# AdaLN attention and FFN on one core: softmax steps regrouped, attention given four PSUM banks of its own, one small product issued earlier

## The chip, the cores and the metric

The kernel runs on one core of one Trainium2 chip. The metric is the device time of one execution in microseconds (us). Three runs of the kernel before gave 823.74, 823.77 and 821.97 us, so the median is 823.74 us.

## The reference, cut to what matters

Input x is 32 sequences of 32 tokens of width 512, 1024 tokens in all. Everything is float32. Two residual blocks follow each other:

```
h    = cond(x)                              # per batch, a 32x32 mix of its tokens
q,k,v = h@Wq+bq, h@Wk+bk, h@Wv+bv           # 512 -> 4096, i.e. 32 heads of 128
q,k  = rms_norm(q,gq), rms_norm(k,gk)       # one norm over all 4096 columns
p    = softmax(q k^T / sqrt(128))           # 32x32 per head and sequence
x    = x + (p v) @ Wo + bo                  # 4096 -> 512
y    = causal convolution of x along the 512 features with a kernel K,
       K = 2 Re(sum_n Ct exp(dtA*l)), masked by length
x    = x + y@kernel + bias + LoRA(y)
```

## The kernel before, in words

Full precision products are made from two halves: every float32 operand is split into a rounded part ("hi", made by ScalarE) and the rest ("lo", made by VectorE), and TensorE runs hi·hi, hi·lo and lo·hi. The program is a hand-written order of instructions for each engine; the engines meet only at semaphores. An engine that waits holds back all that stands behind the wait in its own order. PSUM has eight banks of 512 floats.

The stages by the time of the profiled execution: the projections of q and k, head by head, with the raw scores (to 359 us); the value projection (359 to 518 us); attention and output projection in eight units (518 to 760 us); the convolution and the FFN (to the end).

**Value stage.** It has 28 steps, i = 7t + j with four groups t and seven products j of a Strassen scheme. In each step TensorE does two pairs of products (`value_pair`, L795 to L797). In step i VectorE makes the lo half of the weights for a later step (`split_value`, L1578), then adds each pair's result into `v_sb` (`value_post`, L1642 to L1662); at j = 0 there is nothing to add there, since ScalarE copies (`first_out`). TensorE's first product of group t needs the adds of step j = 5 of the group before (`vc22_ok`, `vu3_ok`, L1658 and L1659). Between these steps VectorE also does the inverse norms (after the adds of step 9), `soft_max(0)` (after step 11), `soft_norm(0)` (after step 13) and `spread(0)` (after step 24). GpSimd makes the weight sums of group t (`value_sums(t)`, L624 to L632) and, around them, the angle and exponent tables of the convolution kernel (`reduce_angles`, `exponents`); when all that is done it clears `p_blocks` (L683). `value_sums(t)` waits for splits 7t and 7t + 1 of VectorE.

**Softmax of a unit.** A unit n is eight heads times half of the tokens. Its work on VectorE is `soft_max(n)` (scale, row maximum, subtract: L1697, L1701, L1703), then ScalarE's exponential (`exp_scores(n)`, L1344), then `soft_norm(n)` (row sum, reciprocal, scale: L1708, L1710, L1712), then `spread(n)` (four transposes into the block matrix `p_blocks`, L1723). There is one buffer `sm_s` and one `p_blocks`: `soft_max(n)` waits for `spread(n-1)`, and `spread(n)` waits until TensorE has used `p_blocks` for unit n - 1.

**Attention of a unit.** TensorE: `attend(n)` makes eight outputs u (L1032) in four banks, `PV_BANK`, used in turn. ScalarE rounds each into `at_hi` (L1352), VectorE makes `at_lo` (L1762), and output u of unit n may start only when `at_lo` of output u - 4 is there (`alo_ok`). Then `project_first(n)` (L1049 to L1051, four groups, heads 0 to 3) and `project_second(n, g)` (L1061 to L1063, heads 4 to 7) fill banks 4 to 7, and VectorE adds bank g to `acc` (`accumulate`, L1776), which needs `wo_mm`, one count for each `project_second(n, g)`. Before an even unit the weights of the output projection are split: `split_o(m, 0)` is needed by `project_first(2m)`, `split_o(m, 1)` by `project_second(2m)` (ScalarE L1360, VectorE L1730).

**The small product.** 32 small matmuls (L1072) give the convolution kernel from `u_tab` and `expo`; they stand in front of `attend(1)`, write bank 0, and ScalarE copies the result to `k_sb` (L1403) when GpSimd has added `bo` to all of `acc` (`acc_set`). `attend(1)` waits for that copy at its third output.

VectorE's order for unit 1 in the kernel before is

```
attn_out(1); spread(2); soft_max(3); accumulate(1,(0,)); soft_norm(3)
accumulate(1,(1,)); split_o(1,0); accumulate(1,(2,3)); attn_out(2)
```

and ScalarE's is attn_out(1), exp_scores(3), split_o(1,0), attn_out(2).

Of the kernel before, what the change touches and what calls it, by code (L numbers as in the profile page):

```python
# [29 lines left out]
P = 128  # L30
# [11 lines left out]
NQ = HEADS // QUAD  # L42
OCT = 8
PAIR_BANK = (2, 4, 0, 6)
PV_BANK = (2, 3, 0, 1)
GROUP_ORDER = (3, 0, 1, 2)
UNITS = ((3, 1), (3, 0), (0, 0), (0, 1), (1, 0), (1, 1), (2, 0), (2, 1))
HG = G // 2
# [21 lines left out]
def build_program(nc, x, cond_idx, lengths, cond_w, wq, bq, wk, bk, wv, bv, wo, bo, gq, gk,  # L70
# [3 lines left out]
    with ctx:  # L74
# [19 lines left out]
        def bank(n, width=512):  # L94
            return psum[:, n * 512:n * 512 + width]
# [214 lines left out]
        def _(sp):  # L310
# [110 lines left out]
                sp.dma_start(la_nat[quadrant(c)], lora_a[:, :, P * c:P * c + P].rearrange("n r f -> r n f")).then_inc(la_in, 16)  # L421
            for c in range(KC):
                sp.dma_start(lb_nat[:, c], lora_b.rearrange("n (c p) r -> c p n r", p=P)[c]).then_inc(lb_in, 16)
            load_unit(2)
            sp.wait_ge(kern_d, 4)
            for q in range(4):
                sp.dma_start(kpad[8 * q:8 * q + 8, 0:FEAT].rearrange("h (a c) -> a h c", a=CA),
                             k_sb[32 * q:32 * q + CA]).then_inc(kpad_out, 16)
            next_weights(1)
            load_unit(3)  # L430
            load_unit(4)
# [355 lines left out]
        def _(pe):  # L787
# [221 lines left out]
            def attend(n):  # L1009


                pe.wait_ge(p_ok, n + 1)
                if n == 0:
                    pe.wait_ge(vc12_ok, 8)
                    pe.wait_ge(vc22_ok, 8)
                    pe.wait_ge(vu3_ok, 8)
                elif n == 1:
                    pe.wait_ge(vc11_ok, 8)
                    pe.wait_ge(vc21_ok, 8)
                else:  # L1020
                    pe.wait_ge(vu_in, 16 * (n - 1))
                for u in range(OCT):
                    part = (1 if u < QUAD else 0) + (2 if n == 0 else 0)
                    cols = slice(HD * (u % QUAD), HD * (u % QUAD) + HD)
                    if n == 0 and u == 2:
                        pe.wait_ge(vc21_ok, 7)
                    if not (n == 0 and u < 4):
                        pe.wait_ge(alo_ok, OCT * n + (u - 3))
                    if n == 1 and u == 2:
                        pe.wait_ge(kern_ok, 1)  # L1030
                    for g in range(HG):
                        last = mm(bank(PV_BANK[u % 4])[:, P * g:P * g + P], v_sb[:, part, g, cols], p_blocks[:, u, g, :],  # L1032
                                  start=True, stop=True)
                    last.then_inc(pv_mm, 1)

            def project_first(n):


                at_hi, at_lo = attn(n)
                pe.wait_ge(wolo_ok, 2 * (n // 2) + 1)  # L1040
                pe.wait_ge(alo_ok, OCT * n + QUAD)
                for g in range(HG):
                    if n == 0:
                        pe.wait_ge(vc21_ok, 8)
                    else:
                        pe.wait_ge(acc_ok, HG * (n - 1) + g + 1)
                    tok = slice(P * g, P * g + P)
                    for h in range(QUAD):
                        mm(bank(4 + g), at_hi[:, h, tok], wo_hi_a[:, h, :], start=(h == 0), stop=False)  # L1049
                        mm(bank(4 + g), at_hi[:, h, tok], wo_lo_a[:, h, :], start=False, stop=False)  # L1050
                        last = mm(bank(4 + g), at_lo[:, h, tok], wo_hi_a[:, h, :], start=False, stop=False)  # L1051
                last.then_inc(wo_half, 1)

            def project_second(n, g):

                at_hi, at_lo = attn(n)
                pe.wait_ge(wolo_ok, 2 * (n // 2) + 2)
                pe.wait_ge(alo_ok, OCT * n + OCT)
                tok = slice(P * g, P * g + P)
                for h in range(QUAD):  # L1060
                    mm(bank(4 + g), at_hi[:, QUAD + h, tok], wo_hi_b[:, h, :], start=False, stop=False)  # L1061
                    mm(bank(4 + g), at_hi[:, QUAD + h, tok], wo_lo_b[:, h, :], start=False, stop=False)  # L1062
                    last = mm(bank(4 + g), at_lo[:, QUAD + h, tok], wo_hi_b[:, h, :], start=False, stop=(h == QUAD - 1))  # L1063
                last.then_inc(wo_mm, 1)

            for n in range(7):
                if n == 1:
                    pe.wait_ge(tab_ok, 1)
                    pe.wait_ge(alo_ok, OCT * n)
                    for h in range(SEQ):  # L1070
                        i, q = h // 4, h % 4
                        last = mm(bank(0)[32 * q:32 * q + CA, CL * i:CL * i + CL], u_tab[:, :, 8 * q + i],  # L1072
                                  expo[:, 0:CL, 8 * q + i], start=True, stop=True, tile_position=(0, 32 * q))
                    last.then_inc(kern_mm, 1)
                attend(n)
                project_first(n)
                for g in range(HG):
                    project_second(n, g)

            def transpose_x2(g):  # L1080

                pe.wait_ge(acc_ok, HG * 6 + g + 1)
                if g >= 4:
                    pe.wait_ge(x2p_ok, g - 3)
                for c in range(KC):
                    last = nc.tensor.transpose(bank(g % 4)[:, P * c:P * c + P], acc[:, g, P * c:P * c + P], ident[:, :])
                last.then_inc(xt_mm, 1)

            attend(7)
# [84 lines left out]
        def _(act):  # L1174
# [206 lines left out]
            for i in range(1, 28):  # L1381
                t, j = i // 7, i % 7
                if j == 0:
                    split_value(i + 2)
                if i + 3 < 28 and j != 6:
                    split_value(i + 3)
                if j == 0:
                    first_out(t, 0)
                    first_out(t, 1)
                if i == 12:  # L1390
                    exp_scores(0)
                if i == 24:
                    tables()
            split_o(0, 0)


            for n in range(8):
                if n == 1:
                    act.wait_ge(kern_mm, 1)
                    act.wait_ge(acc_set, G)  # L1400
                    for q in range(4):
                        rows = slice(32 * q, 32 * q + CA)
                        last = sc.activation(k_sb[rows].rearrange("a h c -> a (h c)"), bank(0, 8 * CL)[rows, :], ACT.Copy)  # L1403
                    last.then_inc(kern_ok, 1)
                attn_out(n)
                if n % 2 == 0:
                    split_o(n // 2, 1)
                if n == 0:
                    exp_scores(1)
                if n + 2 < 8:  # L1410
                    exp_scores(n + 2)
                if n % 2 == 1 and n < 7:
                    split_o(n // 2 + 1, 0)


            def x2_out(g):

                act.wait_ge(xt_mm, g + 1)
                sc.activation(x2p[:, :, :, BPG * g:BPG * g + BPG].rearrange("p s c b -> p c b s"),
                              bank(g % 4).rearrange("p (c b s) -> p c b s", c=KC, b=BPG), ACT.Copy).then_inc(x2p_ok, 1)  # L1420

            for g in range(G):
                x2_out(g)
# [35 lines left out]
        def _(dve):  # L1459
# [276 lines left out]
            for i in range(1, 28):  # L1736
# [2 lines left out]
                    split_value(i + 2)  # L1739
                if i + 3 < 28 and j != 6:  # L1740
                    split_value(i + 3)
                if i == 27:
                    split_o(0, 0)
                if j > 0:
                    for pair in range(2):
                        value_post(t, j, pair)
                if i == 9:
                    inverse_norms()
                if i == 11:
                    soft_max(0)  # L1750
                if i == 13:
                    soft_norm(0)
                if i == 24:
                    spread(0)

            def attn_out(n):

                at_hi, at_lo = attn(n)
                for u in range(OCT):
                    h = OCT * UNITS[n][0] + u  # L1760
                    dve.wait_ge(ahi_ok, OCT * n + u + 1)
                    v.scalar_tensor_tensor(at_lo[:, u, :], bank(PV_BANK[u % 4]), params[:, PARAM["bv"], h:h + 1],  # L1762
# [2 lines left out]
            def accumulate(n, groups):  # L1765

                group, half = UNITS[n]
                for g in groups:
# [4 lines left out]
                        before = (0, 0, 1, 0, 2, 3, 4, 5)[n]  # L1773
                        dve.wait_ge(acc_ok, HG * before + g + 1)
                    at = HG * half + g
                    v.tensor_tensor(acc[:, at, :], bank(4 + g), acc[:, at, :], ALU.add).then_inc(acc_ok, 1)  # L1776

            for n in range(8):
                attn_out(n)
                if n == 0:  # L1780
                    soft_max(1)
                if n % 2 == 0:
                    split_o(n // 2, 1)
                if n == 0:
                    soft_norm(1)
                if n + 1 < 8:
                    spread(n + 1)
                if n + 2 < 8:
                    soft_max(n + 2)
                if n == 7:  # L1790
                    dve.wait_ge(lora, 2 * (2 * NLORA - 1))
                    v.transpose(a_turn[:].rearrange("p g c r -> p (g c) r"), a_sum[:].rearrange("p g (c f) -> p (g c) f", f=32)).then_inc(turned, 1)
                    v.transpose(b_turn[:].rearrange("p g c o -> p (g c) o"), b_sum[:].rearrange("p g c r -> p (g c) r")).then_inc(turned, 1)
                accumulate(n, (0,))
                if n + 2 < 8:
                    soft_norm(n + 2)
                accumulate(n, (1,))
                if n % 2 == 1 and n < 7:
                    split_o(n // 2 + 1, 0)
                accumulate(n, (2, 3))  # L1800
# [76 lines left out]
```

## Time and profile before

| what | value |
|---|---|
| profiled execution, its own time | 823.41 us |
| its span (first to last instruction) | 821.2 us |
| mean granted TensorE clock | 0.996 of full speed |
| VectorE busy | 647.0 us (79%) |
| GpSimd busy | 525.8 us (64%) |
| ScalarE busy | 327.9 us (40%) |

The span cut in 40 slices, each digit the busy share in tenths (slices 17 to 25 are the value stage, 25 to 37 attention):

```profile
PE   8799999999999999999998999999999999999998
DVE  5989898888888888987799776998998898751442
ACT  4555555555555555582223224322412421322520
POOL 4988983333333333429989997967999999910430
```

PE is TensorE, DVE VectorE, ACT ScalarE, POOL GpSimd. The 2.2 us between span and time lie outside the traced instructions.

### The profile page before, as it was taken

What the parts mean: (1) busy time and instruction counts of PE and PEld (TensorE: products, weight loads), DVE (VectorE), ACT (ScalarE), POOL (GpSimd) and SP (SyncE); (2) the same over time, 40 slices, a digit from 0 to 9 for tenths busy, and PEclk for the clock granted to TensorE, in tenths of its full rate; (3) what the DMA queues carried; (4) which work ended last, traced back from release to release, by engine and by line L of the source; (5) the groups of instructions that cost most, each with busy time, mean ns of one, the idle gap of its engine ahead of it and who ended that gap; (6) DMA issues with size and microseconds to landing.
All of it is one profiled execution on the core that took longest, in us unless ns stands there. A gap on an engine that the chain in (4) does not pass through costs nothing. (4 is left out here: it accounts for less than half of the span.)

```text
span 821.2 us, 15207 instructions
## 1 busy us (share of the span) xinstructions
PE 803.1 (98%) x6089; PEld 658.5 (80%) x6089; DVE 647.0 (79%) x652; ACT 327.9 (40%) x371; POOL 525.8 (64%) x457
## 2 busy tenths in 40 slices
PE   8799999999999999999998999999999999999998
PEld 7587888888888888888887888887888888888476
DVE  5989898888888888987799776998998898751442
ACT  4555555555555555582223224322412421322520
POOL 4988983333333333429989997967999999910430
PEclk9999999999999999999999999999999999999999
DMA  5132111111111111304433531419404724418501
GB/s 174 51 75 60 51 51 51 51 51 51 51 51 51 50 46 46 113 2 154 191 136 136 178 128 53 167 31 184 164 36 154 259 100 154 154 41 261 123 26 77
DMA packets 80703, 81.80 MB, mean 100 GB/s; under 512 B 26028, under 2 KB 61196, under 8 KB 78620
## 3 DMA queue, kind: packets, MB, share of 16 engines
q1 hardware_dynamic: 79872, 81.16, 30.9%
q8 instruction: 25, 0.41, 0.2%
q10 hardware_dynamic: 796, 0.15, 0.1%
q14 instruction: 10, 0.08, 0.0%
HBM read 64.90 MB, written 16.40 MB: 99 GB/s over the span
## 5 line engine op out<-in xcount | busy, mean ns | idle before, releaser
L494 POOL TENSOR_TENSOR w_raw<-w_raw 128x256 f32<-128x256 f32 x32 | 44.1, 1380 | 136.1 <-DMA w_raw<-in_wk 135.5
L848 PE MATMUL psum<-t_hi,w_hi 128*128 128x512 f32 x256 | 103.7, 405 | 3.2 <-DVE qk_sb L1562 1.4
L849 PE MATMUL psum<-t_lo,w_hi 128*128 128x512 f32 x256 | 99.7, 389 | 0.0
L850 PE MATMUL psum<-t_hi,w_lo 128*128 128x512 f32 x256 | 99.6, 389 | 0.0
L1313 ACT ACTIVATE sq<-qk_sb 128x1024 f32<-128x1024 f32 x31 | 32.9, 1062 | 142.9 <-issue 133.7
L1570 DVE TENSOR_TENSOR sumsq<-sumsq,sq 128x1024 f32<-128x1024 f32 x62 | 80.8, 1304 | 0.0
L848 PE MATMUL psum<-mix_hi,w_hi 128*128 128x512 f32 x192 | 74.9, 390 | 2.1 <-ACT params L1224 1.1
L850 PE MATMUL psum<-mix_hi,w_lo 128*128 128x512 f32 x192 | 74.7, 389 | 0.0
L849 PE MATMUL psum<-mix_lo,w_hi 128*128 128x512 f32 x192 | 74.7, 389 | 0.0
L1352 ACT ACTIVATE at_hi<-psum,params 128x512 fp32r<-128x512 f32 x64 | 43.9, 688 | 69.8 <-PE psum L1032 69.7
L1032 PE MATMUL psum<-p_blocks,v_sb 128*128 128x128 f32 x512 | 61.1, 281 | 3.2 <-DVE at_lo L1762 1.8
L1032 PEld LDWEIGHTS psum<-p_blocks,v_sb 128*128 128x128 f32 x512 | 60.2, 196 | 4.7 <-DVE at_lo L1762 2.0
L1476 DVE TENSOR_TENSOR w_lo<-w_raw,w_hi 128x1792 fp32r<-128x1792 f32 x30 | 61.4, 2047 | 0.0
L1203 ACT ACTIVATE w_hi<-w_raw 128x1792 fp32r<-128x1792 f32 (+2 forms) x34 | 54.8, 1611 | 13.2 <-issue 6.8
L848 PEld LDWEIGHTS psum<-t_hi,w_hi 128*128 128x128 f32 x256 | 48.0, 187 | 14.9 <-DVE t_lo L1528 2.8
L850 PEld LDWEIGHTS psum<-t_hi,w_lo 128*128 128x128 f32 x256 | 48.1, 188 | 10.5
L1762 DVE SCALAR_TENSOR_TENSOR at_lo<-psum,params,at_hi 128x512 fp32r<-128x512 f32 x64 | 47.2, 748 | 11.2 <-ACT at_hi L1352 5.2
L849 PEld LDWEIGHTS psum<-t_lo,w_hi 128*128 128x128 f32 x256 | 48.1, 188 | 8.6
L1049 PE MATMUL psum<-wo_hi_a,at_hi 128*128 128x512 f32 x128 | 50.5, 395 | 0.0
L795 PE MATMUL psum<-ring_hi,t_hi 128*128 128x512 f32 x128 | 49.9, 390 | 0.3 <-DVE v_sb L1655 0.3
L1061 PE MATMUL psum<-wo_hi_b,at_hi 128*128 128x512 f32 x128 | 50.1, 391 | 0.0
L1051 PE MATMUL psum<-wo_hi_a,at_lo 128*128 128x512 f32 x128 | 49.8, 389 | 0.0
(278 smaller groups left out, 2124.3 us busy)
## 6 DMA issues: line engine op xcount, KB each, us to landing
v_sb<-v_scr_dram SPq DMA_DIRECT2D x6, 2048.0 KB, 8.0
v_scr_dram<-v_sb SPq DMA_DIRECT2D x9, 1024.0 KB, 3.9
w_raw<-in_wq SPq DMA_DIRECT2D x32, 256.0 KB, 2.9
w_raw<-in_wk SPq DMA_DIRECT2D x32, 256.0 KB, 3.2
wv_raw<-in_wv SPq DMA_DIRECT2D x16, 512.0 KB, 4.3
toep<-kpad_dram SPq DMA_DIRECT2D x2, 4096.0 KB, 14.3
wo_raw_a<-in_wo SPq DMA_DIRECT2D x4, 1024.0 KB, 5.4
wo_raw_b<-in_wo SPq DMA_DIRECT2D x4, 1024.0 KB, 5.4
```

Source lines behind the costliest of these rows:

```text
L795: mm(out, lh, rh, start=(n == 0), stop=False)
L848: mm(bank(n), wh, hi[:, c, tok], start=(i == 0), stop=False)
L849: mm(bank(n), wh, lo[:, c, tok], start=False, stop=False)
L850: last = mm(bank(n), wl, hi[:, c, tok], start=False, stop=(i == 1))
L1032: last = mm(bank(PV_BANK[u % 4])[:, P * g:P * g + P], v_sb[:, part, g, cols], p_blocks[:, u, g, :], start=True, stop=True)
L1049: mm(bank(4 + g), at_hi[:, h, tok], wo_hi_a[:, h, :], start=(h == 0), stop=False)
L1051: last = mm(bank(4 + g), at_lo[:, h, tok], wo_hi_a[:, h, :], start=False, stop=False)
L1061: mm(bank(4 + g), at_hi[:, QUAD + h, tok], wo_hi_b[:, h, :], start=False, stop=False)
L1203: return sc.activation(w_hi[slot][:, lo:hi, :].rearrange("p b n -> p (b n)"), w_raw[slot][:, lo + 1:hi + 1, :].rearrange("p b n -> p (b n) ...
L1476: v.tensor_tensor(w_lo[slot][:].rearrange("p b n -> p (b n)"), w_raw[slot][:, 1:8, :].rearrange("p b n -> p (b n)"), w_hi[slot][:].rearran ...
L1570: v.tensor_tensor(sumsq[:, m, :], sumsq[:, m, :], sq[:, m, :], ALU.add).then_inc(total, 1)
L1762: v.scalar_tensor_tensor(at_lo[:, u, :], bank(PV_BANK[u % 4]), params[:, PARAM["bv"], h:h + 1], at_hi[:, u, :].bitcast(F32), ALU.add, ALU. ...
```

## The change

- `PV_BANK` becomes (2, 3, 4, 5); the output projection gets `O_BANK` = (0, 1, 6, 7). `attend(0)` no longer waits for `vc21_ok`. The transposes after attention use `PV_BANK` too.
- In the value stage the inverse norms, `soft_max(0)` and `soft_norm(0)` move to steps 7, 14 and 21, ahead of where that step's adds would stand (there are none); `exp_scores(0)` follows at step 16. `spread(0)` stands ahead of the adds of step 25, which is the place it had.
- VectorE's `split_o(0, 0)` moves behind the last adds of the value stage and the first four `at_lo` of unit 0.
- The small product moves between `project_first(0)` and `project_second(0)` and writes bank 4; its copy moves behind `exp_scores(1)` on ScalarE. `load_unit(2)` moves behind the writes of `kpad` in the DMA queue.
- VectorE's order for units 0 and 1 is written out, and from unit 2 on `soft_norm(n+1)` stands in unit n rather than `soft_norm(n+2)`.

```diff
-PV_BANK = (2, 3, 0, 1)
+PV_BANK = (2, 3, 4, 5)
+O_BANK = (0, 1, 6, 7)
...
-            load_unit(2)
             sp.wait_ge(kern_d, 4)
...
+            load_unit(2)
             next_weights(1)
...
-                    if n == 0 and u == 2:
-                        pe.wait_ge(vc21_ok, 7)
...
+            def kern():
+
+                pe.wait_ge(tab_ok, 1)
+                pe.wait_ge(alo_ok, OCT)
+                for h in range(SEQ):
+                    i, q = h // 4, h % 4
+                    last = mm(bank(4)[32 * q:32 * q + CA, CL * i:CL * i + CL], u_tab[:, :, 8 * q + i],
+                              expo[:, 0:CL, 8 * q + i], start=True, stop=True, tile_position=(0, 32 * q))
+                last.then_inc(kern_mm, 1)
+
             for n in range(7):
...
                 attend(n)
                 project_first(n)
+                if n == 0:
+                    kern()
...
-                if i == 12:
+                if i == 16:
                     exp_scores(0)
...
+            def kern_out():
+
+                act.wait_ge(kern_mm, 1)
+                act.wait_ge(acc_set, G)
...
             for n in range(8):
...
                 attn_out(n)
                 if n % 2 == 0:
                     split_o(n // 2, 1)
+                if n < 2:
+                    exp_scores(n + 1)
                 if n == 0:
-                    exp_scores(1)
-                if n + 2 < 8:
+                    kern_out()
+                if 0 < n < 6:
                     exp_scores(n + 2)
                 if n % 2 == 1 and n < 7:
                     split_o(n // 2 + 1, 0)
...
-                if i == 27:
-                    split_o(0, 0)
+                if i == 7:
+                    inverse_norms()
+                if i == 14:
+                    soft_max(0)
+                if i == 21:
+                    soft_norm(0)
+                if i == 25:
+                    spread(0)
                 if j > 0:
                     for pair in range(2):
                         value_post(t, j, pair)
-                if i == 9:
-                    inverse_norms()
-                if i == 11:
-                    soft_max(0)
-                if i == 13:
-                    soft_norm(0)
-                if i == 24:
-                    spread(0)
...
-            for n in range(8):
+            attn_out(0, range(QUAD))
+            split_o(0, 0)
+            attn_out(0, range(QUAD, OCT))
+            split_o(0, 1)
+            soft_max(1)
+            soft_norm(1)
+            spread(1)
+            accumulate(0, range(HG))
+            attn_out(1)
+            soft_max(2)
+            accumulate(1, (0,))
+            soft_norm(2)
+            spread(2)
+            soft_max(3)
+            accumulate(1, (1,))
+            split_o(1, 0)
+            accumulate(1, (2, 3))
+            for n in range(2, 8):
                 attn_out(n)
-                if n == 0:
-                    soft_max(1)
                 if n % 2 == 0:
                     split_o(n // 2, 1)
-                if n == 0:
-                    soft_norm(1)
-                if n + 1 < 8:
+                if n < 7:
+                    soft_norm(n + 1)
                     spread(n + 1)
                 if n + 2 < 8:
                     soft_max(n + 2)
...
-                accumulate(n, (0,))
-                if n + 2 < 8:
-                    soft_norm(n + 2)
-                accumulate(n, (1,))
+                accumulate(n, (0, 1))
```

## Rows read from the trace of the kernel before

**Rows 1.** The page's first part: busy time (share) and instructions of each engine.
```profile
PE 803.1 (98%) x6089; PEld 658.5 (80%) x6089; DVE 647.0 (79%) x652; ACT 327.9 (40%) x371; POOL 525.8 (64%) x457
```

**Rows 2.** Waits of TensorE: who waited for whom, us in total, times, longest.
```profile
PE psum L795 <- DVE v_sb L1659: 2.3, 1, 2.3
...
PE psum L1032 <- DVE at_lo L1762: 1.8, 1, 1.8
...
PE psum L1032 <- DVE v_sb L1662: 1.2, 1, 1.2
...
PE psum L795 <- DVE v_sb L1655: 0.3, 1, 0.3
```

**Rows 3.** TensorE in order of time: start, us, operation, [idle before].
```profile
518.46 2.02 PE L1032 MATMUL psum<-p_blocks,v_sb 128*128 128x128 f32 x16
...
527.08 0.48 PE L1049 MATMUL psum<-wo_hi_a,at_hi 128*128 128x512 f32 x1
...
549.03 1.14 PE L1072 MATMUL psum<-expo,prod 128*16 128x32 f32 x64
```

**Rows 4.** Stretches of time: length, busy by engine, granted clock, DMA.
```profile
437.49:447.10 9.61, 7.36 (x26) 5.79 (x26) 9.54 (x10) 2.00 (x3) 9.03 (x7) 0.82 0.54 220
...
550.10:561.40 11.30, 9.30 (x72) 8.95 (x65) 8.90 (x13) 6.69 (x12) 4.72 (x6) 0.85 1.16 156
```

**Rows 5.** The chain of waits that ended last: start, us, engine, tile, line.
```profile
434.08 3.42 DVE ring_lo L1578
437.64 2.36 POOL wv_raw L632
...
502.85 3.47 POOL p_blocks L683
...
583.43 7.27 PE psum L1032 x64
```

**Rows 6.** GpSimd in order of time, value stage.
```profile
427.33 2.41 POOL L624 TENSOR_TENSOR wv_raw<-wv_raw 128x1024 f32<-128x1024 f32 x1 [3.06 <-issue]
...
448.79 1.50 POOL L665 TENSOR_SCALAR prod<-turns 128x512 f32<-128x512 f32 x1
...
451.74 2.35 POOL L665 TENSOR_SCALAR prod<-turns 128x512 f32<-128x512 f32 x1
...
497.44 1.96 POOL L666 TENSOR_TENSOR ang<-ang,prod 128x352 f32<-128x352 f32 x1
```

**Rows 7.** VectorE in order of time, end of the value stage and units 1 and 2.
```profile
506.42 4.99 DVE L1723 STREAM_TRANSPOSE p_blocks<-sm_s 32x1024 f32<-32x1024 f32 x4 [3.53 <-POOL p_blocks L683]
...
517.10 1.21 DVE L1659 TENSOR_TENSOR v_sb<-psum,v_sb 128x1024 f32<-128x1024 f32 x1
...
563.07 4.98 DVE L1723 STREAM_TRANSPOSE p_blocks<-sm_s 32x1024 f32<-32x1024 f32 x4
...
575.31 0.69 DVE L1776 TENSOR_TENSOR acc<-psum,acc 128x512 f32<-128x512 f32 x1 [2.11 <-PE psum L1063]
...
577.55 3.48 DVE L1712 TENSOR_TENSOR sm_s<-sm_s,row_inv 128x1024 f32<-128x1024 f32 x1
...
586.07 6.14 DVE L1762 SCALAR_TENSOR_TENSOR at_lo<-psum,params,at_hi 128x512 fp32r<-128x512 f32 x8
```

**Rows 8.** Durations by line: ns min/median/max, first and last start.
```profile
L1712 DVE TENSOR_TENSOR sm_s<-sm_s,row_inv x8: 1224/1728/3479, 445.8 to 693.4; 128x1024 f32<-128x1024 f32 x8
...
L1697 DVE TENSOR_TENSOR sm_s<-scores,inv_norm x8: 1225/2275/2859, 429.4 to 683.9; 128x1024 f32<-128x1024 f32 x8
...
L1703 DVE TENSOR_TENSOR sm_s<-sm_s,row_max x8: 1226/1812/2192, 432.1 to 687.5; 128x1024 f32<-128x1024 f32 x8
...
L1730 DVE TENSOR_TENSOR wo_lo_a<-wo_raw_a,wo_hi_a x4: 2281/3113/3402, 518.2 to 695.7; 128x2048 fp32r<-128x2048 f32 x4
```

**Rows 9.** ScalarE in order of time, unit 1.
```profile
573.23 1.06 ACT L1344 ACTIVATE sm_s<-sm_s 128x1024 f32<-128x1024 f32 x1 [10.86 <-DVE sm_s L1703]
578.09 1.92 ACT L1360 ACTIVATE wo_hi_a<-wo_raw_a 128x2048 fp32r<-128x2048 f32 x1 [3.79 <-DMA wo_raw_a<-in_wo]
```

## What the change is expected to do

> **What bounds the kernel now.** I read the busy shares first: TensorE is at work for 98% of the span, VectorE for 79% [rows 1]. Nothing here makes TensorE's work shorter, since no matmul is added or dropped. So the change can only give back idle time or time at a low clock, and it can add both. Next come TensorE's waits: 2.3 us for L1659 of the value stage, 1.8 us for `at_lo`, 1.2 us for L1662, 0.3 us for L1655 [rows 2]. Then the stretches round the two long ones. At the start of group t = 2 (9.61 us) TensorE is busy for 7.36 us at a mean granted clock of 0.82: 2.25 us idle and about 0.18 x 9.61 = 1.7 us lost at the lower level, 4.0 us in all. `attend(1)` takes 11.30 us at 0.85 where the undisturbed `attend(2)` takes 7.27: 4.0 us lost, of which about 1.7 by the clock [rows 4, 5]. Last the chain of waits, which shows that the value stage has a second master beside TensorE. It runs VectorE L1578 (3.42 us), GpSimd L632 at 437.64, GpSimd without a break to its clearing of `p_blocks` (starts 502.85), VectorE's `spread(0)` and adds, TensorE [rows 5]. VectorE stood idle 3.53 us before `spread(0)`, waiting for that clearing [rows 7].
>
> **The change part by part.**
>
> Value stage. With the inverse norms at step 7, and `soft_max(0)` out of step 11, VectorE is in time for group 2, and the stall with its clock loss goes: -4.0 us at step 14. What is late next is GpSimd. Its `value_sums(2)` began at 427.33 after 3.06 us of idle time [rows 6], waiting for `split_value(14)`, and its last part waited for the 3.42 us split that stood behind `soft_max(0)`. Both splits now come in time. Its first two sums can fill that idle time, the third waits for TensorE's step 12, so L632 starts when two sums of 2.4 us are through: about 434.7 instead of 437.64, 2.9 us earlier [rows 5]. From there GpSimd is never idle until `p_blocks` is cleared. But `soft_max(0)` now lies beside it, with two operations that read SBUF twice, as the splits do. A GpSimd operation of one kind takes 1.50 or 2.35 us [rows 6]; beside 13 such VectorE operations between 440 and 503 us, nine GpSimd operations are longer than their like, from the one at 451.74 to the one at 497.44, by 7.5 us together: 0.6 us for each VectorE operation. Two more cost 1.2 us (bounds 0 and 2 x 0.86 = 1.7). The clearing ends 2.9 - 1.2 = 1.7 us earlier, while TensorE would be 4.0 us earlier, and before it had 0.3 us of wait there already. So TensorE meets a new stall of about 0.3 + 4.0 - 1.7 = 2.6 us in front of the last step. That is as long as the one removed, and I charge the same 1.7 us of clock. Gain of the stage: 1.7 - 1.7 = 0, or up to 0.3 if the adds overlap better; I take 0.3. Bounds: +3.0 us gained (no contention, no clock loss, the adds end it) and 0.6 lost.
>
> On that contention the trace shows the prices above [rows 6]. The Trainium skill, "SBUF — State Buffer", section "Who interferes with whom", says that a VectorE instruction with two SBUF inputs contends with a GpSimd one that reads SBUF, and that the second to issue blocks until the first is through. By it the two added operations could hold GpSimd for their full length, some 2.4 us, and the total would be about 1.2 us more; the mean above is what I use.
>
> `attend(0)`. From its start to the first projection it takes 527.08 - 518.46 = 8.62 us [rows 3] against 7.27: 1.35 us over, by the wait for L1662 [rows 2]. With banks 2 to 5 that wait goes. But `split_o(0, 0)` (2.28 to 3.40 us [rows 8]) now stands behind the fourth `at_lo`. That one ends some 5.3 us after the start (four outputs of 7.27/8 = 0.91 us, then ScalarE and VectorE with 0.7 and 0.75), so the split ends at 7.6 to 8.7, where the projection wants it at 7.27. New wait 0.3 to 1.4 us, 0.7 taken. Gain 0.7 (0 to 1.1).
>
> The small product. Its 32 matmuls (64 records) take 1.1 us wherever they stand [rows 3]. At the new place `tab_ok` is some 8 us old, and the copy ends before `attend(1)` needs bank 4: nothing. `load_unit(2)` waits for `attend(1)` in any case, and the writes of `kpad` now ahead of it are issued before that: nothing; the bound is the few us of the landing, against 20 us until the data are wanted. GpSimd starts the LoRA sums about 10 us earlier; they end earlier, and only the durations of [rows 8] beside them may move.
>
> `attend(1)`. VectorE has to finish `split_o(0,0)`, four `at_lo`, `split_o(0,1)`, `soft_max(1)`, `soft_norm(1)`, `spread(1)` before TensorE comes back; with the durations of [rows 8] that ends about 29 us after the start of `attend(0)`, where TensorE wants it at 31. The adds of unit 0 need 2.5 us, mostly before `attend(1)`; the waits of 0.2 and 1.8 us go with their clock: -4.0 us (bounds 4.0 and 2.0, if `spread(1)` is late).
>
> `attend(2)`. Here I expect the cost. `accumulate(1, (0,))` waits for the first `project_second` of unit 1, and `soft_norm(2)`, `spread(2)`, `soft_max(3)`, `split_o(1,0)` are now queued behind it on VectorE, with `exp_scores(3)` and ScalarE's half of `split_o(1,0)` behind `soft_max(3)`, and `attn_out(2)` behind all. Before, `spread(2)` ran from 563.07 and `soft_max(3)` after it, under the projections, and VectorE still had 2.11 us to wait for that accumulate at 575.31 [rows 7]. Now VectorE is idle some 7 us ahead of it instead. In times of the kernel before, with TensorE wanting `attend(2)` at 583.43 [rows 5]:
> - accumulate, row sum, reciprocal: 577.55 - 575.31 = 2.24 [rows 7] -> 577.55
> - the scaling L1712, median 1.73 [rows 8] -> 579.3; `spread(2)` 4.98 [rows 7] -> 584.3. TensorE starts about 1.0 us late.
> - `soft_max(3)`: L1697, L1701, L1703; 573.23 - (563.07 + 4.98) = 5.1 as it ran before [rows 7, 9] -> 589.4
> - ScalarE: exponential 1.06, split 1.92 [rows 9] -> 592.4; VectorE only adds group 1 meanwhile
> - VectorE's split 3.11 [rows 8] -> 595.6; two more adds 1.25 -> 596.8; first `at_lo` 0.75 -> 597.6.
> TensorE's output u = 4 wants that at 583.43 + 7.27/2 = 587.1. It waits until 597.7: 10.6 us later than before, and 1.7 us of clock on top, 12.3 us. Low end: all durations of [rows 8] at their minimum and `soft_max(3)` at 3.75 give 595.1, so 8.0 + 1.7 = 9.7. High end: at their maximum 601.0, and twice the clock loss: 17.3. I take 12.3.
>
> Units 3 to 7. `soft_norm(n+1)` in unit n adds 3 to 5 us ahead of `spread(n+1)`, which before stood done long ahead of its use (563.07 for a use at 583.43 [rows 5, 7]); `attn_out(n+1)` is reached when the last add is, at the time at which TensorE wants it, as before. Nothing (bound: 1 us for each odd unit).
>
> Sum against the profiled execution: -0.3 - 0.7 - 4.0 + 12.3 = +7.3, so 823.41 + 7.3 = 830.7 us; the median of the runs is 0.3 us above that execution, within its scatter. I say 831.
>
> **Rivals.**
> 1. The value stage gains all: if GpSimd keeps up (its operations dodge VectorE's) or the last stall is too short for the clock to fall, 3 us more come back: 828. For it: the 0.3 and 1.2 us waits now have no clock loss. Against: GpSimd has no gap in which to catch up.
> 2. The stall in `attend(2)` costs more: a wait of 9 to 10 us may leave the clock low for longer after it, VectorE meets the LoRA sums at worst, or `spread(1)` is late: 834. The only stalls seen are short ones.
> 3. Not slower: VectorE gets through its new queue at `attend(2)` in the time that TensorE leaves it, so only the gains count: 823.4 - 4.0 - 1.4 - 4.0 = 814. It decides at 587.1: between 575.31 and there VectorE has 11.8 us for work that I price at 22.3. For it: all this work was hidden before, and VectorE has a fifth of its time free. Against: the order on the engine, in which nothing passes a waiting instruction.
>
> **How the numbers follow.** Forecast 0.55, rival 1 0.15, rival 2 0.18, rival 3 0.12. The ends of the sum are 823.4 - 3.0 - 1.1 - 4.0 + 9.7 = 825.0 and 823.4 + 0.6 - 2.0 + 17.3 = 839.3; the range 826 to 836 leaves out rival 3 and the outer part of the others. 0.3% is about what a measurement of this kernel can tell from no change. Faster 0.12, same 0.03, slower 0.85.
>
> **What would show it.** Right: no wait at L795 near 437; a wait of 2 to 3 us at L795 in front of the last value step, with VectorE's `spread(0)` waiting for GpSimd L683 (its number in the new file); `attend(1)` at 7.3 us; VectorE idle 5 to 8 us before `accumulate(1,(0,))`; one wait of TensorE of 8 to 12 us for `at_lo` in `attend(2)`; units 3 to 7 as long as before. Wrong: `attend(2)` undisturbed, or a wait as long in a later unit.

## The result, and the profile after

The changed kernel takes 829.75 us (median of four runs, 828.68 to 832.66) against 823.75: a ratio of 1.0085, 95% interval 1.0069 to 1.0102. On another chip it gave 830.25 us and 1.0078 (1.0064 to 1.0092). It is 6.0 us slower, as forecast in sign and nearly in size. Its profiled execution, 832.66 us, is the longest of the four; 1.45 us of that lies ahead of the value stage's step 7 (400.86 us against 399.41), where the two kernels do not differ, so the stages below are compared by their lengths.

| stretch | before, us | after, us | difference | forecast |
|---|---|---|---|---|
| value stage from step 7 to `attend(0)` | 119.05 | 115.44 | -3.6 | -0.3 |
| `attend(0)` | 8.62 | 8.67 | 0.0 | -0.7 |
| `attend(1)` | 11.30 | 7.06 | -4.2 | -4.0 |
| `attend(2)`, from where TensorE wants it | 7.27 | 22.37 | +15.1 | +12.3 |

The sum is +7.3 us. The forecast's terms also add up to +7.3; that both sums are the same is luck, since two of the terms missed by some 3 us in opposite directions. Behind these stages the kernels run alike: from `project_first(2)` on, each unit takes 28.9 us in both.

Line numbers are now those of the changed kernel: L1031 is `attend` (L1032 before), L1048 `project_first`, L1060 to L1062 `project_second`, L1704 to L1710 `soft_max`, L1715 to L1719 `soft_norm`, L1730 `spread`, L1737 VectorE's split, L1767 `at_lo`, L1781 `accumulate`, L633 the last weight sum, L684 the clearing. TensorE's waits after (who waited for whom, us in total, times, longest) answer to [rows 2]:

```profile
PE psum L1031 <- DVE at_lo L1767: 9.9, 1, 9.9
PE psum L1031 <- DVE p_blocks L1730: 2.2, 1, 2.2
...
PE psum L1048 <- DVE wo_lo_a L1737: 1.3, 1, 1.3
...
PE psum L796 <- DVE v_sb L1662: 0.8, 1, 0.8
```

The 2.3, 1.8 and 1.2 us waits are gone; two new ones, both in unit 2, make 12.1 us, and the third is new too. Read next what VectorE did there, in order of time (start, us, operation, [idle before, what ended it]), against [rows 7]:

```profile
556.89 2.30 DVE L1704 TENSOR_TENSOR sm_s<-scores,inv_norm 128x1024 f32<-128x1024 f32 x1
559.23 1.22 DVE L1708 TENSOR_REDUCE row_max<-sm_s 128x32 f32<-128x1024 f32 x1
560.48 2.05 DVE L1710 TENSOR_TENSOR sm_s<-sm_s,row_max 128x1024 f32<-128x1024 f32 x1
569.12 0.69 DVE L1781 TENSOR_TENSOR acc<-psum,acc 128x512 f32<-128x512 f32 x1 [6.58 <-PE psum L1062]
569.73 1.21 DVE L1715 TENSOR_REDUCE row_sum<-sm_s 128x32 f32<-128x1024 f32 x1
570.97 0.35 DVE L1717 RECIPROCAL row_inv<-row_sum 128x32 f32<-128x32 f32 x1
571.35 2.97 DVE L1719 TENSOR_TENSOR sm_s<-sm_s,row_inv 128x1024 f32<-128x1024 f32 x1
574.36 4.99 DVE L1730 STREAM_TRANSPOSE p_blocks<-sm_s 32x1024 f32<-32x1024 f32 x4
579.38 2.70 DVE L1704 TENSOR_TENSOR sm_s<-scores,inv_norm 128x1024 f32<-128x1024 f32 x1
...
587.86 3.42 DVE L1737 TENSOR_TENSOR wo_lo_a<-wo_raw_a,wo_hi_a 128x2048 fp32r<-128x2048 f32 x1 [2.32 <-ACT wo_hi_a L1363]
591.20 1.28 DVE L1781 TENSOR_TENSOR acc<-psum,acc 128x512 f32<-128x512 f32 x2
592.40 2.71 DVE L1767 SCALAR_TENSOR_TENSOR at_lo<-psum,params,at_hi 128x512 fp32r<-128x512 f32 x4
```

`soft_max(2)` is done at 562.5; VectorE then stands idle 6.58 us until TensorE ends its first `project_second` of unit 1, and from there has 23.3 us of queue before the first `at_lo` of unit 2 (569.12 to 592.40), where before it had 10.8 (575.31 to 586.07 [rows 7]). TensorE, in order of time:

```profile
579.40 3.84 PE L1031 MATMUL psum<-p_blocks,v_sb 128*128 128x128 f32 x32 [2.16 <-DVE p_blocks L1730]
...
593.19 6.50 PE L1031 MATMUL psum<-p_blocks,v_sb 128*128 128x128 f32 x32 [9.95 <-DVE at_lo L1767]
599.45 0.48 PE L1048 MATMUL psum<-wo_hi_a,at_hi 128*128 128x512 f32 x1
```

The first four outputs take 3.84 us, the four after the long wait 6.50: 2.7 us more for the same matmuls. The stretches (length, busy by engine, granted clock, DMA) give the reason and answer to [rows 4]:

```profile
437.49:447.10 9.61, 9.61 (x45) 7.93 (x43) 8.91 (x7) 4.06 (x4) 9.18 (x7) 1.00 0.66 254
548.16:555.22 7.06, 7.06 (x65) 7.06 (x64) 5.29 (x8) 4.74 (x7) 6.82 (x4) 1.00 0.54 68
577.08:599.45 22.37, 10.26 (x66) 9.91 (x65) 17.11 (x16) 7.22 (x9) 21.74 (x9) 0.77 0.15 48
593.20:599.00 5.80, 5.80 (x28) 5.80 (x29) 3.41 (x5) 1.66 (x3) 5.56 (x4) 0.52 0.01 3
```

The first two are what the change won: step 14 and `attend(1)` are full of work at full clock. The last, behind the long wait, is at about the lower level (1.2 GHz, a granted 0.50) all through.

In the value stage GpSimd and VectorE read (answering to [rows 5 to 7]):

```profile
436.24 2.42 POOL L633 TENSOR_TENSOR wv_raw<-wv_raw,ring_raw 128x1024 f32<-128x1024 f32 x1
...
500.63 3.52 POOL L684 MEMSET p_blocks<- 128x4096 f32 x1
```

```profile
504.25 4.99 DVE L1730 STREAM_TRANSPOSE p_blocks<-sm_s 32x1024 f32<-32x1024 f32 x4 [4.05 <-POOL p_blocks L684]
509.27 2.36 DVE L1662 TENSOR_TENSOR v_sb<-psum,v_sb 128x1024 f32<-128x1024 f32 x2
```

VectorE still waits for the clearing, 4.05 us now, and TensorE for the adds behind it, 0.82 us.

### The profile page after: what moved, and what is told of

It reads as the page before. It is cut to its first block, busy times and chain, and to the rows that moved or that the text cites. A ratio compares the mean times of both kernels' runs of the same rounds, so it can differ in the third digit from the quotient of the medians.

```text
span 830.5 us, 15207 instructions
## 1 busy us (share of the span) xinstructions
PE 804.4 (97%) x6089; PEld 658.8 (79%) x6089; DVE 647.5 (78%) x652; ACT 327.3 (39%) x371; POOL 520.8 (63%) x457
## 4 chain that ended last, share of the span: by engine, by line
PE 74%; POOL 15%; DVE 7%; issue 2%; ACT 2%; POOLq 0%; DVEq 0%
PE psum L849 13%; PE psum L851 12%; PE psum L850 12%; PE psum L1031 6%; PE psum L1048 4%; PE psum L1050 4%; PE psum L1049 3%; PE psum L1060 3%; PE psum L1062 3%; PE psum L1061 3%; PE psum L884 3%; POOL prod L666 3%; POOL ang L667 2%; PE psum L796 1%; PE psum L797 1%
## 5 line engine op out<-in xcount | busy, mean ns | idle before, releaser
L1031 PE MATMUL psum<-p_blocks,v_sb 128*128 128x128 f32 x512 | 61.6, 283 | 12.1 <-DVE at_lo L1767 9.9
L1031 PEld LDWEIGHTS psum<-p_blocks,v_sb 128*128 128x128 f32 x512 | 61.0, 199 | 13.5 <-DVE at_lo L1767 10.1
L1206 ACT ACTIVATE w_hi<-w_raw 128x1792 fp32r<-128x1792 f32 (+2 forms) x34 | 54.8, 1613 | 12.1 <-issue 6.8
L1767 DVE SCALAR_TENSOR_TENSOR at_lo<-psum,params,at_hi 128x512 fp32r<-128x512 f32 x64 | 47.3, 748 | 13.6 <-ACT at_hi L1355 7.6
L1048 PE MATMUL psum<-wo_hi_a,at_hi 128*128 128x512 f32 x128 | 50.5, 395 | 1.3 <-DVE wo_lo_a L1737 1.3
L1060 PE MATMUL psum<-wo_hi_b,at_hi 128*128 128x512 f32 x128 | 50.2, 392 | 0.0
L1049 PE MATMUL psum<-wo_lo_a,at_hi 128*128 128x512 f32 x128 | 49.8, 389 | 0.0
```

The costliest lines, as they stand in the source:

```text
L1048: mm(bank(O_BANK[g]), at_hi[:, h, tok], wo_hi_a[:, h, :], start=(h == 0), stop=False)
L1049: mm(bank(O_BANK[g]), at_hi[:, h, tok], wo_lo_a[:, h, :], start=False, stop=False)
L1060: mm(bank(O_BANK[g]), at_hi[:, QUAD + h, tok], wo_hi_b[:, h, :], start=False, stop=False)
L1206: return sc.activation(w_hi[slot][:, lo:hi, :].rearrange("p b n -> p (b n)"), w_raw[slot][:, lo + 1:hi + 1, :].rearrange("p b n -> p (b n) ...
```

## The experiments

All times are medians. Each ratio is against the kernel before on the same chip, with its 95% interval; it is estimated from all runs and so differs a little from the quotient of two medians. The kernel before gave a median of 823.19 us on the chip of e1 to the first e4, 823.88 on that of after_again, e8, e9 and e10, and 823.05 on that of e4_again, e11 and e12. "Unit 2 loss" is the time from `project_first(1)` to `project_first(2)`, less the 28.95 us that it takes undisturbed (28.94 in e3_value_only, 28.95 in e8_both): 15.3 us in the changed kernel (555.22 to 599.45), 14.7 when it ran again. Beside it stands the time from the start of `attend(0)` to the end of the span: 302.7 us before, 314.2 and 313.2 in the two traces of the changed kernel.

**The order of unit 1, undone in the changed kernel (e1_order).**

```diff
-            accumulate(1, (0,))
             soft_norm(2)
             spread(2)
             soft_max(3)
-            accumulate(1, (1,))
+            accumulate(1, (0, 1))
```

> The changed kernel with one edit: VectorE does soft_norm(2), spread(2), soft_max(3) ahead of accumulate(1,(0,)) again. Theory (the queue behind that accumulate makes the stall in attend(2)): both waits there (2.2 and 9.9 us) and the clock loss go, attend(2) takes 7.3 us, some 15 us less than the changed kernel, so about 815 us, 1% below the kernel before. Rival (other parts of the change carry the loss: banks, the product's place, LoRA sums earlier): at most 3 us less, 826 or more.

Measured 823.88 us, ratio 1.0014 (1.0000 to 1.0027); unit 2 loss 7.1 us. Some half of the loss went and half stayed, between both expectations (304.9 us from `attend(0)` to the end, 8 to 9 us less; the medians, each against the kernel before, give 5 to 6). VectorE was never idle for the accumulate now, and yet late:

```profile
561.41 1.22 DVE L1715 TENSOR_REDUCE row_sum<-sm_s 128x32 f32<-128x1024 f32 x1 [1.13 <-ACT sm_s L1347]
...
565.66 4.99 DVE L1730 STREAM_TRANSPOSE p_blocks<-sm_s 32x1024 f32<-32x1024 f32 x4
570.68 2.75 DVE L1704 TENSOR_TENSOR sm_s<-scores,inv_norm 128x1024 f32<-128x1024 f32 x1
...
583.79 2.71 DVE L1767 SCALAR_TENSOR_TENSOR at_lo<-psum,params,at_hi 128x512 fp32r<-128x512 f32 x4
```

`spread(2)` begins 10 us after `attn_out(1)` ends (555.57), since `soft_max(2)`, the exponential and `soft_norm(2)` come first. In the kernel before these three were done in unit 0, and `spread(2)` followed at once. So there was a second cause that I had not separated: the change puts two softmaxes into unit 1.

**The same order put into the kernel before (e2_late_in_before).** Banks, value stage and product stay as they were, and `soft_max(2)` in unit 0.

```diff
+                if n == 1:
+                    accumulate(1, (0,))
+                    soft_norm(2)
                 if n + 1 < 8:
                     spread(n + 1)
...
-                accumulate(n, (0,))
-                if n + 2 < 8:
+                if n != 1:
+                    accumulate(n, (0,))
+                if 0 < n < 6:
                     soft_norm(n + 2)
```

> The kernel before with only that order: in unit 1 VectorE does accumulate(1,(0,)) and soft_norm(2) ahead of spread(2) and soft_max(3); value stage, banks, product as before. Theory: the same stall appears in attend(2), +13 to +16 us, so 837 to 840 us, with VectorE idle 6 to 8 us before the accumulate. Rival: the stall needs the other parts too; within 3 us of the kernel before.

Measured 836.55 us, ratio 1.0161 (1.0138 to 1.0184), unit 2 loss 15.6 us; the wait is `PE psum L1032 <- DVE at_lo L1762: 12.8`. VectorE (line numbers of the kernel before) was idle for 12.15 us ahead of the accumulate, not for the 6 to 8 that I expected, because `soft_max(2)` was already done:

```profile
571.63 0.69 DVE L1776 TENSOR_TENSOR acc<-psum,acc 128x512 f32<-128x512 f32 x1 [12.15 <-PE psum L1063]
...
588.60 2.52 DVE L1712 TENSOR_TENSOR sm_s<-sm_s,row_inv 128x1024 f32<-128x1024 f32 x1
...
596.15 2.71 DVE L1762 SCALAR_TENSOR_TENSOR at_lo<-psum,params,at_hi 128x512 fp32r<-128x512 f32 x4
```

The order alone makes a stall of the full size, without the other parts of the change. The queue is not quite the same one: it takes 24.5 us against 23.3, since `soft_norm(3)` (the line at 588.60 is its end) still stands in it, while VectorE no longer waits for ScalarE's half of the split. The time is 0.5 us below my band, which had left out the shorter `attend(1)`. That stretch took 7.56 us in this kernel instead of 11.30: without `soft_norm(2)` among the adds of unit 0 VectorE reached `attn_out(1)` in time. So most of that gain of the change belongs to VectorE's order too, not to banks or product; the 0.2 us wait for the copy of the product stays here.

**Value stage alone, in the kernel before (e3_value_only).**

```diff
+                if i == 7:
+                    inverse_norms()
+                if i == 14:
+                    soft_max(0)
+                if i == 21:
+                    soft_norm(0)
+                if i == 25:
+                    spread(0)
```

(the old places removed, `exp_scores(0)` at step 16)

> The kernel before with only the value-stage moves: inverse norms, soft_max(0), soft_norm(0) at steps 7, 14, 21, exp_scores(0) at 16. As the prediction had it (GpSimd 1.7 us earlier, last stall with clock loss): gain 0 to 0.3 us. As the trace of the changed kernel reads (stage shorter by 3.6 us: 119.05 to 115.44): gain 3 to 4 us, 820 us, ratio 0.996. split_o(0,0) still stands in front of the last adds here, so the 1.2 us wait in attend(0) stays.

Measured 819.55 us, ratio 0.9955 (0.9937 to 0.9973): the reading of the trace after holds, my forecast of this term does not. Its value stage from step 7 is 116.14 us, 2.9 less than before. (The wait at the last value step was 1.5 us here and in e1_order, with a stage of 116.15 us there, and 0.8 us in the changed kernel.) Another 1.6 us in `attend(1)` is clock, of which 0.8 us is left at the end: from `project_first(3)` to `project_first(5)` it took 0.6 us longer than the kernel before. `attend(1)` has the same waits as in the kernel before, yet its stretch, to be laid beside the second of [rows 4], is

```profile
547.21:556.88 9.67, 7.67 (x71) 7.31 (x65) 8.90 (x13) 6.69 (x12) 3.26 (x5) 1.00 1.10 159
```

at full clock, where before the same 1.8 us wait was followed by a granted 0.85.

**ScalarE's half of the split first (e4_act_split_first, and again as e4_again).** ScalarE only: `split_o(1, 0)` ahead of `exp_scores(3)`.

```diff
+                if n == 1:
+                    split_o(1, 0)
                 if 0 < n < 6:
                     exp_scores(n + 2)
-                if n % 2 == 1 and n < 7:
+                if n % 2 == 1 and 1 < n < 7:
```

> The changed kernel with ScalarE's half of split_o(1,0) ahead of exp_scores(3). Theory: VectorE waited 2.3 us for that half behind the exponential, so the wait of attend(2) for at_lo is 2.0 to 2.5 us shorter (9.9 to 7.6) and the time 2 to 3 us less, about 827. Rival (VectorE's own queue alone sets it): no change.

> Once more the changed kernel with ScalarE's half of split_o(1,0) ahead of exp_scores(3), since its trace showed shorter waits (7.5 and 1.5 us against 9.9 and 1.3 to 2.2) and its first time no clear gain. Theory: 1.5 to 3 us less than the changed kernel, ratio 1.004 to 1.006. Rival: no gain, 1.0075 to 1.0085.

Measured 829.51 us, ratio 1.0072 (1.0049 to 1.0094), and again 827.70 us, 1.0073 (1.0049 to 1.0096). The traces show the wait at 7.5 instead of 9.9 us both times and a unit 2 loss of 11.7 and 11.5 us, 3 us less. The times do not settle it: 1.0073 lies between my two bands, and the intervals hold both a gain of 2 us and none. The traces speak for the gain: from `attend(0)` to the end they take 310.4 and 310.7 us, 2.5 to 3.9 us less than the two of the changed kernel.

**The changed kernel again (after_again)**, for the chip on which the next three ran.

> The changed kernel once more, to be compared on this chip with the next ones. All theories: 829 to 831 us, ratio 1.007 to 1.010.

Measured 830.25 us, ratio 1.0078.

**Both edits (e8_both).** Beside the first, `soft_max(2)` goes back to unit 0, with the adds of unit 0 between the `at_lo` of unit 1.

```diff
             spread(1)
-            accumulate(0, range(HG))
-            attn_out(1)
             soft_max(2)
-            accumulate(1, (0,))
+            accumulate(0, (0, 1))
+            attn_out(1, range(QUAD))
+            accumulate(0, (2, 3))
+            attn_out(1, range(QUAD, OCT))
             soft_norm(2)
             spread(2)
             soft_max(3)
-            accumulate(1, (1,))
+            accumulate(1, (0, 1))
```

> The changed kernel with two edits in VectorE's order: soft_norm(2), spread(2), soft_max(3) ahead of accumulate(1,(0,)), and soft_max(2) back in unit 0, with the adds of unit 0 put between the at_lo of unit 1. Theory, as the first edit alone recovered only half (attend(2) 14.2 us against 22.4 and 7.3): the other half is soft_max(2) and the exponential behind it, which the change moved into unit 1; with both undone attend(2) takes 7.3 us and the time is 814 to 816 us, ratio 0.989 to 0.991. Rival (what remains of the stall is slower VectorE operations beside the LoRA sums, which start 13 us earlier): 819 us or more.

Measured 816.87 us, ratio 0.9918 (0.9904 to 0.9931), unit 2 loss 0, and 299.4 us from `attend(0)` to the end. VectorE, for comparison with the lines of the changed kernel:

```profile
556.48 1.20 DVE L1715 TENSOR_REDUCE row_sum<-sm_s 128x32 f32<-128x1024 f32 x1
...
560.70 4.99 DVE L1730 STREAM_TRANSPOSE p_blocks<-sm_s 32x1024 f32<-32x1024 f32 x4
...
574.27 3.49 DVE L1737 TENSOR_TENSOR wo_lo_a<-wo_raw_a,wo_hi_a 128x2048 fp32r<-128x2048 f32 x1 [1.73 <-ACT wo_hi_a L1363]
577.69 1.27 DVE L1781 TENSOR_TENSOR acc<-psum,acc 128x512 f32<-128x512 f32 x2
578.88 6.22 DVE L1767 SCALAR_TENSOR_TENSOR at_lo<-psum,params,at_hi 128x512 fp32r<-128x512 f32 x8
```

The operations beside the LoRA sums are as long as in e1_order (3.49 us for the split after 3.46, 2.57 us for L1719 after 2.57), and the stall is gone all the same, so the rival falls. The exact time is 1 us above my band, partly for a wait of 0.44 us that the new place of the adds makes in `attend(1)`.

**Only the second edit (e11_max_early)** (`soft_max(2)` early, the accumulate still ahead):

```diff
             spread(1)
-            accumulate(0, range(HG))
-            attn_out(1)
             soft_max(2)
+            accumulate(0, (0, 1))
+            attn_out(1, range(QUAD))
+            accumulate(0, (2, 3))
+            attn_out(1, range(QUAD, OCT))
             accumulate(1, (0,))
             soft_norm(2)
```

> The changed kernel with only the second edit of e8_both: soft_max(2) back in unit 0; accumulate(1,(0,)) stays ahead of soft_norm(2). Theory (the accumulate anchors the queue at TensorE's first project_second of unit 1, whatever is done before it): attend(2) loses 14 to 15 us as in the changed kernel, 829 to 831 us, no gain. Rival (the two edits add, 8 us and 7 us): attend(2) some 7 us shorter, 822 to 824 us.

Measured 828.98 us, ratio 1.0073 (1.0055 to 1.0090), unit 2 loss 14.2 us. The line that decides is VectorE's accumulate:

```profile
567.06 0.69 DVE L1781 TENSOR_TENSOR acc<-psum,acc 128x512 f32<-128x512 f32 x1 [11.89 <-PE psum L1062]
```

5 us of work taken from in front of the wait only made the wait 5 us longer (6.58 to 11.89). The edits do not add: the second is worth 7 us once the first is made, and within 1 us of nothing without it. The expectation holds, the rival does not.

**The product back (e9_product_back)** in front of `attend(1)`, its copy in front of `attn_out(1)`, from e8_both:

```diff
             for n in range(7):
+                if n == 1:
+                    kern()
                 attend(n)
                 project_first(n)
-                if n == 0:
-                    kern()
```

> e8_both with the small product back in front of attend(1) and its copy back in front of attn_out(1) on ScalarE. Theory: the product costs the same 1.1 us at both places, but the copy holds ScalarE 1.5 us when at_hi of unit 1 is wanted, so attend(1) waits at output 4 for about 1.5 us and perhaps loses clock: +1 to +3 us against e8_both. Rival: hidden, within 0.5 us.

Measured 816.57 us, ratio 0.9918 (0.9904 to 0.9931), the same as e8_both: the rival holds. `attend(1)` had no wait at all. The product's place is worth nothing that shows.

**`split_o(0, 0)` back (e12_split_back)** in front of the last adds, from e8_both:

```diff
+                if i == 27:
+                    split_o(0, 0)
...
-            attn_out(0, range(QUAD))
-            split_o(0, 0)
-            attn_out(0, range(QUAD, OCT))
+            attn_out(0)
```

> e8_both with split_o(0,0) back in front of the last adds of the value stage, banks as changed. Theory: the wait of 1.3 us at project_first(0) goes, but the split and the adds hold the first at_lo to about 5 us after the start of attend(0), so TensorE waits 1 to 2 us at output 4 instead: within 1 us of e8_both, 816 to 818. Rival (new banks alone are enough to free this place): 1.3 us less, 815.5.

Measured 817.09 us, ratio 0.9936 (0.9922 to 0.9951), against 816.87 and 0.9918 on another chip: within 1 us by the medians, with intervals that overlap, and the rival's 1.3 us less is not there. The waits swap as expected: the projection's goes, and this comes:

```profile
520.32 3.84 PE L1031 MATMUL psum<-p_blocks,v_sb 128*128 128x128 f32 x32 [1.22 <-DVE at_lo L1769]
```

**The clearing first (e10_clear_first)**, from e8_both: GpSimd clears `p_blocks` ahead of its last exponents.

```diff
+            pool.wait_ge(wvlo_ok, 28)
+            gp.memset(p_blocks[:], 0.0).then_inc(blocks_zero, 1)
             exponents(32, 48)
             gp.memset(sm("t2"), 0.0).then_inc(ang_ok, 1)
-            pool.wait_ge(wvlo_ok, 28)
-            gp.memset(p_blocks[:], 0.0).then_inc(blocks_zero, 1)
```

> e8_both with GpSimd's clearing of p_blocks ahead of its last exponents. Theory (GpSimd's clearing sets the end of the value stage): it ends 1.8 us earlier, the wait in front of the last value step (1.5 us) goes, and the time is 1 to 2 us less than e8_both; the tables come later but have 8 us to spare. Rival (VectorE's adds set it): no change.

Measured 816.42 us, ratio 0.9907 (0.9892 to 0.9922), the lowest of all but within the interval of e8_both, so that the 1 to 2 us that I expected are not shown in the time. In the trace the wait at the last value step is gone and the stage is 1.2 us shorter (114.24 against 115.44), so the clearing does set its end; 0.6 us of that comes back as a longer wait for `split_o(0, 0)`:

```profile
523.73 0.51 PE L1048 MATMUL psum<-wo_hi_a,at_hi 128*128 128x512 f32 x1 [1.95 <-DVE wo_lo_a L1737]
```

## Why the prediction was right, and where it was not

- **Sign and size.** 831 was forecast, 829.75 measured. The mechanism of the loss was right and measured by itself; that the number came so close is luck in part. The value stage won 3.3 us more than I gave it and `attend(2)` lost 2.8 us more, and the two errors cancel.
- **Value stage, gain 0.3.** L633 began at 436.24 - 1.45 = 434.8 on the clock of before, where I had 434.7, and the clearing does set the end (e10_clear_first). Two sizes were off. I added 1.2 us for two more VectorE operations beside GpSimd; from the end of the sums to the end of the clearing GpSimd took 65.5 us (438.60 to 504.15) after 66.4 before, so the price was not there. With that the last stall was 0.8 us instead of 2.6 (the sign that I had named, a wait of 2 to 3 us there, did not come), and no low clock followed it (granted 1.00 over the stage), for which I had charged 1.7. At 3.6 us the gain came out beyond the end that I had bounded at 3.0. That was rival 1, together with a larger stall in unit 2 (rival 2).
- **`attend(0)`, gain 0.7.** The 1.2 us wait turned into the wait for `split_o(0, 0)`, 1.29 us, at the upper end of my bounds. With the split at its old place, e12_split_back shows a wait of 1.22 us at output 4 instead. The wait also differs from run to run: 1.3 us in five traces with this part alike, 0.2 us in three (the last section says why), so 0.7 lies between two outcomes.
- **`attend(1)`, gain 4.0.** Right at 4.2, and e2_late_in_before shows by which edit: VectorE's order of unit 0. Only the 2.0 us of waits are sure in it: e3_value_only had the same waits as the kernel before without the low clock behind them, so the 1.7 us of clock may or may not be lost.
- **Product and `load_unit(2)` at nothing.** Right for the product (e9_product_back); the DMA's place was not tried by itself, and no wait in unit 2 names it.
- **`attend(2)`, loss 12.3.** The place and the anchor were right: queue behind `accumulate(1,(0,))`, idle VectorE ahead of it (6.58 us, "some 7"), two waits of 2.2 and 9.9 us for 1.0 and 9.6 (10.6 less the late start). The size was short mainly in L1719 (2.97 us for a median of 1.73) and in the clock, 2.7 us for 1.7.
- **What I left out.** The step "now VectorE is idle some 7 us ahead of it instead" took that order for the only fault. e1_order recovered 8 of 15 us of the unit 2 loss: behind it stood `soft_max(2)` with its exponential, moved from unit 0 to unit 1. e11_max_early shows why it did not show in the sum: it lay in the shadow of the wait. The number did not need it, the remedy did.
- **Rival 3** is out: VectorE needed 23.3 us where 11.8 were free.

The version with both edits undone keeps what the change wins and beats both kernels: 816.87 us, 0.8% below the kernel before.

## What to carry to other kernels

In a hand-written order, find for each wait, also of an engine that is not the bottleneck, what stands behind it, and give that work its time from the moment of the wait, not from when the engine comes free: 15 us were lost here with VectorE idle for 6.6 us just ahead. Undoing one cause may bring only part back, because a second lies in its shadow; try both edits singly and together (of the loss in unit 2, 1 and 8 us alone and 15 together; by the medians, each against the kernel before, under 1, 5 to 6, and 13). A busy share of 78% says nothing on whether a given queue of 23 us fits a hole of 12.

## What was not expected of the hardware

- A wait of 1.8 us in front of the same matmuls was followed by the lower clock in the kernel before (granted 0.85 over the stretch, 1.7 us lost) and not in e3_value_only (1.00). The runs of one and the same kernel differ too: the 18 of the kernel before on the chip of e1 to e4 had mean granted clocks from 0.996 to 1.000, and the three longest (825.4 to 826.1 us) all had 0.996. The clock loss of a short stall is a chance here, not a term to be counted in full. The Trainium skill, "TensorE: Matmul & The Clock Gate", section "What's actually happening", says that the number of matmuls at the low clock at the start of a kernel varies from run to run; the rows here show such a variation inside a kernel.
- The four outputs after the long waits took 5.63 us (wait 5.1, e1_order), 6.09 and 5.96 (7.5, the two e4 runs), 6.50, 6.78 and 6.68 (9.9 to 10.0, the changed kernel twice and e11_max_early) and 5.57 (12.8, e2_late_in_before) against 3.84 undisturbed: 1.7 to 2.9 us, and the longest wait cost least.
- `split_o(0, 0)` took 3.38 us in the changed kernel and 2.28 in e1_order, with the same program up to there; TensorE's wait behind it was 1.3 us and 0.2 us, and `attend(0)` 8.67 and 7.58 us. In the changed kernel a GpSimd operation had begun at 521.49, the split at 521.53: GpSimd's took its usual 1.27 us and the split 1.1 us more, and GpSimd's next one (522.84) took 3.23 us for a usual 1.28. In e1_order they began at 521.29 and 521.31, and the split took its 2.28 us and GpSimd's 3.46. The split was long in after_again, e8_both and both e4 runs too, and short in e9_product_back and e11_max_early. So VectorE pays in some runs and not in others, by an order that differs from run to run. The Trainium skill, "SBUF — State Buffer", section "Who interferes with whom", says that issue order decides who blocks; these rows agree that one side waits until the other is through (521.29 + 1.27 + 2.28 = 524.84, and GpSimd's ended at 524.75), though the start times do not tell which: GpSimd's began first, by 0.01 to 0.06 us, in all eight traces.
